# An eight-batch attention and expert tower on one core: queries and keys projected three heads ahead instead of two, in the third and fourth unit of a head

## What is computed

```python
q  = concat(qn, rope(qr))            # per head 32 + 64, from the latent cq
k1 = concat(kn, rope(kr))            # causal branch, kr shared by the heads
ks = rope_part(sel @ Wsel_k)         # 128 selected tokens
kw = rope_part(x @ Wwin_k)           # window of 128 tokens
o  = g0 * attn(q, k1, causal) + g1 * attn(q, ks) + g2 * attn(q, kw, causal & window)
out = o.reshape(B, T, NH * VD) @ Wproj
```

## Time and profile before

| | us |
|---|---|
| median of three runs (1845.43 to 1846.01) | 1845.62 |
| the profiled execution, its own time | 1848.94 |
| its span | 1847.0 |
| PE busy in the span | 1430.7 (77%) |
| DVE busy | 1437.1 (78%) |
| ACT busy | 1222.9 (66%) |
| POOL busy | 1434.9 (78%) |
| POOL's share of the chain that ended last | 58% |
| from one batch's transfer of latents to the next's, six times (191.02 to 191.58) | 191.2 |

### The profile page before, as it was taken

How to read it: one execution, slowest core, us unless ns; L and a number is a source line. 1 busy time by engine, 2 the same in 40 slices (tenths; PEclk the granted TensorE clock), 3 DMA queues, 4 the chain that set the end, 5 groups by cost and what they waited for, 6 DMA issues and landing times.

```text
span 1847.0 us, 64237 instructions
## 1 busy us (share of the span) xinstructions
PE 1430.7 (77%) x19368; PEld 1152.9 (62%) x19368; DVE 1437.1 (78%) x4982; ACT 1222.9 (66%) x3280; POOL 1434.9 (78%) x2126
## 2 busy tenths in 40 slices
PE   1041488888888888888888888888888888888778
PEld 0021377767776777777777767677767776766643
DVE  5737588877888788878887888788878887878845
ACT  0041378767777777768776777687768776767634
POOL 6775489877887798779887998698868887889710
PEclk9985699999999999999999999999999999999989
DMA  5110232313222322222222222222222221333200
GB/s 92 22 26 2 47 63 51 58 38 65 54 54 41 65 53 51 44 61 52 58 50 55 53 55 51 54 51 55 55 50 55 51 57 38 55 64 68 53 4 21
DMA packets 327554, 92.04 MB, mean 50 GB/s; under 512 B 321104, under 2 KB 323024, under 8 KB 327520
## 3 DMA queue, kind: packets, MB, share of 16 engines
q1 hardware_dynamic: 324448, 88.48, 24.3%
q0 software_dynamic: 3072, 3.15, 1.0%
HBM read 6.51 MB, written 1.05 MB: 4 GB/s over the span
## 4 chain that ended last, share of the span: by engine, by line
POOL 58%; issue 20%; DVE 8%; PE 7%; POOLq 3%; DMA 2%; ACT 1%; DVEq 0%; ACTq 0%; SPq 0%
POOL big L425 10%; POOL big L424 8%; POOL kparts L460 6%; POOL big L394 5%; POOL vh L480 4%; POOL kparts L457 4%; POOL qparts L446 4%; POOL kk L428 3%; POOL kk L429 3%; POOL qs L428 3%; POOL qs L429 3%; POOL osum L473 2%; DVE S L1008 2%; DMA qh<-qparts 1%; DVE big L1018 1%
## 5 line engine op out<-in xcount | busy, mean ns | idle before, releaser
L635 ACT ACTIVATE big<-S,negm 128x128 f32<-128x128 f32 (+3 forms) x1536 | 575.9, 448 | 209.3 <-DVE negm L1008 208.9
L647 ACT ACTIVATE big<-PT 128x384 f16<-128x384 f32 (+3 forms) x1024 | 426.7, 454 | 133.0 <-PE PT L1373 98.4
L1018 DVE SCALAR_TENSOR_TENSOR big<-PT,big 128x384 f16<-128x384 f32 (+3 forms) x1024 | 472.1, 500 | 32.5 <-ACT big L647 18.7
L1008 DVE CUSTOM_DVE_ANT_0 S<-S,mask_c,unscale 128x128 f32<-128x128 f32 (+3 forms) x512 | 285.0, 557 | 179.4 <-PE S L1348 167.5
L1348 PE MATMUL S<-k1T,qh 128*128 128x128 f16 (+3 forms) x1536 | 298.6, 304 | 117.2 <-DMA qh<-qparts 107.9
L1348 PE MATMUL S<-kh,qh 128*128 128x128 f16 (+1 forms) x3072 | 324.5, 243 | 0.0
L1395 PEld LDWEIGHTS O<-vh,big 128*128 128x128 f16 x8064 | 274.0, 96 | 46.0 <-DVE big L1030 28.5
L1395 PE MATMUL O<-vh,big 128*128 128x33 f16 x8064 | 283.7, 178 | 19.6 <-DVE big L1030 16.3
L1348 PEld LDWEIGHTS S<-kh,qh 128*128 128x128 f16 x3072 | 231.2, 100 | 56.9 <-issue 1.4
L1380 PE MATMUL PT<-cst,big 128*128 128x128 f32 x1408 | 249.3, 282 | 18.8 <-DVE big L1018 16.1
L1373 PE MATMUL PT<-cst,big 128*128 128x128 f32 x1280 | 233.6, 282 | 18.6 <-DVE big L1018 18.2
(11 more groups left out here) (295 smaller groups left out, 2395.5 us busy)
## 6 DMA issues: line engine op xcount, KB each, us to landing
lat_b<-lat_all SPq DMA_DIRECT2D x8, 448.0 KB, 3.1
qh<-qparts SPq DMA_TRANSPOSE x128, 3.0
kh<-kparts SPq DMA_TRANSPOSE x128, 3.3
xnT_all<-xnT_b SPq DMA_DIRECT2D x14, 128.0 KB, 2.5
xn_b<-xn_all SPq DMA_DIRECT2D x8, 128.0 KB, 2.8
xnT_b<-xnT_all SPq DMA_DIRECT2D x8, 128.0 KB, 2.3
out_dram<-h_all SPq DMA_DIRECT2D x8, 128.0 KB, 2.0
xn_all<-xn_b SPq DMA_DIRECT2D x7, 128.0 KB, 2.0
```

The lines of the kernel that those rows point to most:

```text
L635: last = nc.scalar.activation(pr[par][:, lo:lo + n], S[par][:, lo:lo + n], ACT.Exp, bias=negm[par][:, k:k + 1], scale=-1.0)
L647: last = nc.scalar.activation(pT[par][:, 0, lo:lo + n], PT[:, lo:lo + n], ACT.Copy, scale=PSCALE)
L1008: last = v.tensor_tensor_reduce(out=z, in0=z, in1=m, scale=unscale[:] if k == 0 else kfix[:], scalar=3.0e38, op0=ALU.add, op1=ALU.min, acc ...
L1018: v.scalar_tensor_tensor(pT[par][:, 1, lo:lo + n], PT[:, lo:lo + n], PSCALE, pT[par][:, 0, lo:lo + n], ALU.mult, ALU.subtract).then_inc(s[ ...
```

## The change

`LEAD` gets two more entries, the queries and keys of head 2 (`qp2`, `kp2`). They are projected at the end of the batch before: the queries in unit 3 of its last turn, the keys in `behind` between the scores of the first block and the transposes of the attention's output. In the first batch both stand in `behind`. Inside a batch, turn h now projects head h + 3: its keys in unit 2, its queries in unit 3, and ACT copies them out first in those units; `high_values` moves from unit 2 to unit 1. The loops of PE and ACT take one pair of turns less, and turns 12 and 13 are written out behind them; turn 13 projects nothing. GpSimd does its work in the same order as before, only grouped otherwise in its loop, except that `normalise` in the last batch now stands behind `low_values` and `branch_sum`. DVE and SP are unchanged.

```diff
-        LEAD = ["cq", "qp0", "sel", "k1", "kp0", "qp1", "kp1"]
-        NX = (NH - 2) * 2 + len(LEAD)
+        LEAD = ["cq", "qp0", "sel", "k1", "kp0", "qp1", "kp1", "qp2", "kp2"]
+        NX = (NH - 3) * 2 + len(LEAD)
...
+            def cycle(b, h, par, rows=None, add=True):
                 x = xbase(b) + h * 2
+                low_values(par, b, h + 1)
+                if add:
+                    branch_sum(par, b, h - 1)
                 if rows is not None:
                     normalise(rows, xn_b[:])
-                low_values(1 - par, b, hh - 1)
+                prepare(par, b, h + 3, x + x_index(0, "kp"), x + x_index(0, "qp"))
...
             def heads(b, rows=False):
+                prepare(0, b, 2, xbase(b) + x_lead("kp2"), xbase(b) + x_lead("qp2"))
+                cycle(b, 0, 1, 0 if rows else None, add=False)
                 with g.Fori(0, NH // 2 - 2) as hp:
+                    cycle(b, hp * 2 + 1, 0)
+                    cycle(b, hp * 2 + 2, 1, hp + 1 if rows else None)
+                low_values(0, b, NH - 2)
...
# ACT, turn
-                    if t == 0 and last < 1:
-                        evac_k(p, xb + x_index(0, "kp"), H + 1)
-                    if t == 1 and last < 1:
-                        evac_q(p, xb + x_index(0, "qp"), H + 1)
-                    if t == 2 and last < 2:
+                    if t == 1 and last < 2:
                         high_values(1 - p, b, h + 1)
+                    if t == 2 and xb is not None:
+                        evac_k(1 - p, xb + x_index(0, "kp"), H + 2)
+                    if t == 3 and xb is not None:
+                        evac_q(1 - p, xb + x_index(0, "qp"), H + 2)
...
# PE, turn
-                    if last < 1 and t == 0:
-                        k_proj(h + 2, xb + x_index(0, "kp"))
-                    if last < 1 and t == 1:
-                        q_proj(h + 2, xb + x_index(0, "qp"))
+                    if xb is not None and t == 2:
+                        k_proj(h + 3, xb + x_index(0, "kp"))
+                    if xb is not None and t == 3:
+                        q_proj(h + 3, xb + x_index(0, "qp"))
...
# PE, behind
                 scores(0, 0, 0, H * NT)
+                if first:
+                    lead("qp2", b, nxt)
+                lead("kp2", b, nxt)
```

More of the change, by code:

```diff
@@ L523, in weight_parts, with prepare @@
                 last.then_inc(s["comb_ready"], 1)
-            def prepare(b, h, hh, par, rows=None):
+            def prepare(par, b, hh, xk, xq):
+                key(par, b, hh, xk)
+                query(par, b, hh, xq)
+            def cycle(b, h, par, rows=None, add=True):
                 x = xbase(b) + h * 2
-                key(par, b, hh, x + x_index(0, "kp"))
-                query(par, b, hh, x + x_index(0, "qp"))
+                low_values(par, b, h + 1)
+                if add:
+                    branch_sum(par, b, h - 1)
                 if rows is not None:
                     normalise(rows, xn_b[:])
-                low_values(1 - par, b, hh - 1)
+                prepare(par, b, h + 3, x + x_index(0, "kp"), x + x_index(0, "qp"))
             def heads(b, rows=False):
-                prepare(b, 0, 2, 0, 0 if rows else None)
+                prepare(0, b, 2, xbase(b) + x_lead("kp2"), xbase(b) + x_lead("qp2"))
+                cycle(b, 0, 1, 0 if rows else None, add=False)
                 with g.Fori(0, NH // 2 - 2) as hp:
[L537 to L541, removed]
+                    cycle(b, hp * 2 + 1, 0)
+                    cycle(b, hp * 2 + 2, 1, hp + 1 if rows else None)
+                low_values(0, b, NH - 2)
                 branch_sum(0, b, NH - 4)
@@ L706, in lead @@
                 elif kind[:2] == "qp":
-                    evac_q(int(kind[2]), x, H)
+                    evac_q(int(kind[2]) % 2, x, H if kind != "qp2" else H + 1)
                 elif kind[:2] == "kp":
-                    evac_k(int(kind[2]), x, H)
+                    evac_k(int(kind[2]) % 2, x, H if kind != "kp2" else H + 1)
             def behind(b, nxt, U, first):
@@ L724, in behind @@
                 probs(0, 0, b, U)
+                if first:
+                    lead(LEAD.index("qp2"), nxt, b * NH)
+                lead(LEAD.index("kp2"), nxt, b * NH)
                 if not first:
@@ L729, in behind @@
                 probs(2, 2, b, U + 2)
-            for i in range(len(LEAD)):
+            for i in range(LEAD.index("qp2")):
                 lead(i, 0)
@@ L737, in heads @@
             def heads(b, rows=False):
-                with act.Fori(0, NH // 2 - 1) as hp:
+                with act.Fori(0, NH // 2 - 2) as hp:
                     for p in range(2):
                         turn(b, hp * 2 + p, xbase(b) + hp * 4 + p * 2, p, 0, rows=hp if rows and p == 1 else None)
+                turn(b, NH - 4, xbase(b) + (NH - 4) * 2, 0, 0)
+                turn(b, NH - 3, None, 1, 0, rows=NH // 2 - 2 if rows else None)
             def last_heads(b, nxt):
@@ L1492, in heads @@
             def heads(b, rows=False):
-                with pe.Fori(0, NH // 2 - 1) as hp:
+                with pe.Fori(0, NH // 2 - 2) as hp:
                     for p in range(2):
@@ L1496, in heads @@
                              rows=hp if rows and p == 1 else None)
+                turn(NH - 4, b * NH + NH - 4, xbase(b) + (NH - 4) * 2, 0, 0)
+                turn(NH - 3, b * NH + NH - 3, None, 1, 0, rows=NH // 2 - 2 if rows else None)
             def hidden(b, chunks=(0, 1, 2, 3), between=None):
@@ L1517, in _ @@
             last.then_inc(s["rank_psum"], 1)
-            for kind in LEAD[2:]:
+            for kind in LEAD[2:LEAD.index("qp2")]:
                 lead(kind, 0, 0)
```

## The result

The changed kernel takes 1905.39 us (median of four runs, 1903.54 to 1946.84) against 1845.53: slower, with a ratio of 1.0321 and a 95% interval of 1.0303 to 1.0339. The sign that was forecast and its mechanism, the queries on the chain, are there; the size is not: 59.9 us instead of 26, and the range ended at 1898.

The account below looks back on a forecast made before the run. GpSimd was taken to bound the kernel mid-batch, with the PE, ACT and DVE chain bounding it afterwards. Heads +19, last batch -3 and clock +10 gave +26 on 1848.9, so 1875, or 1872 against the median; range 1838 to 1898.

Parts of the forecast that it names:

- the queries on the chain: Unit 3 on PE: twelve matmuls between `values` and `scores` lengthen the chain through PE, ACT and DVE by 0.74 us.
- What bounds the kernel: Mid-batch, GpSimd sets the pace, busy 9.87 of 10.97 us a head; PE's 107.9 us wait for queries is its lateness.
- The head: One head inside a batch: 10.53 + 0.74 - 0.10 = 11.17 us, longer than GpSimd's 10.97.
- the base of 10.53: Mean length in us of two second-batch heads that GpSimd did not hold, taken as what PE, ACT and DVE need.
- Keys in unit 2: Key projection on PE ahead of unit 2's scores: hidden while `take_hi` holds DVE; taken as 0, bounds 0 and 0.50 us.
- The clock: Ten lower-clock stretches in heads of the first seven batches, 1.9 us each, no longer hidden by GpSimd: 10 us, bounds 0 and 19.
- every second head: Rival: PE's waits in units 0 and 1 make the clock fall in 45 heads, 86 us, 1948 us; chance 0.05.
- Between batches: `kp2` and `qp2` around the end of a batch: hidden by PE's later wait for GpSimd's sums; 0, at most 5.8 us.
- The last batch: GpSimd, which also normalises, stays the limit there; its one wait of 2.89 us can go: taken as -2.9.
- The sum: Whole kernel: 19 - 3 + 10 = +26 us on the profiled 1848.9, giving 1875, or 1872 against the median.
- GpSimd stays the limit: Rival: queries in unit 3 are hidden, heads stay 10.97, GpSimd's waits at batch starts go: -32, 1814 us; chance 0.15.
- The balance rival: Half the queries' time is hidden, a head takes about 10.98 us: 1844 us; below 11.0 the change gains; chance 0.10.

Follow-up runs that it names:

- units01_rolled: Changed kernel with keys projected in unit 0, queries in unit 1, values' copy in unit 2, and turns 12 and 13 back in the loops: 1823.3 us.
- queries1_rolled: Changed kernel with queries back in unit 1, values' copy in unit 3, keys left in unit 2, turns 12 and 13 back in the loops: 1837.6 us.
- queries_later: Changed kernel with turns 12 and 13 back in the loops, unit 3's queries behind its scores and transposes, their copy behind `take_hi`: 1810.7 us.
- later_long: Changed kernel with only unit 3's queries and their copy one step later; turns 12 and 13 stay written out: 1880.2 us.
- units01: Changed kernel with keys projected in unit 0, queries in unit 1, values' copy in unit 2; turns 12 and 13 stay written out: 1891.7 us.

## Why the prediction was wrong in size

**What bounds the kernel**: right. PE's wait for the queries was GpSimd's lateness; it went, and the time went elsewhere.

**The head**: the mechanism was right, and its term nearly so. 11.17 was forecast; heads without a fall take 11.03 in the changed kernel, 11.05 in the one with added work. The queries on the chain cost 0.68 a head (11.05 against 10.37, the mean of the first nine heads in units01_rolled) where 0.64 was put; the base of 10.53, from two heads of the second batch, was 0.16 too long. Since GpSimd held a head at 10.97 before, 0.06 to 0.08 of the 0.68 reaches the time of a head. Keys in unit 2, put at 0, cost at most 0.18 (2.4 in thirteen heads, in queries1_rolled) and nothing that queries_later shows. Wide `maxima` 11.1 to 11.4 apart were to be seen; they are 10.83 and 11.23 apart in turn.

**The clock**: mis-sized. "Ten such stretches", 10 us in all, took the count of the trace before. The count is what changed: 28 instead of 11 in the heads. The 1.9 us put for one was too much: one costs 1.38 us in the pair shown above; against the kernel with the added work they cost 4.1 us a batch, some 25 in six batches. The prediction had the mechanism among its rivals (every second head, 1948 us, chance 0.05) and should have put a lower rate of it into the forecast: the waits that the moved projections leave in units 0 and 1 were named there. The Trainium skill ("TensorE: Matmul & The Clock Gate", "A second HAM failure mode: psum-queue depth-cycling") tells of a kernel in which short idle times between groups of matmuls come often enough to make the clock go up and down; the trace agrees, with waits of 0.85 and 0.66 us ahead of the fall shown.

**Between batches**: this is the step that failed outright. "0, at most 5.8" was worked out for `kp2` and `qp2`, and for those it holds: 24.2 with them and the short program, 24.7 before. That the change writes two turns out stands in the description of the change, and no term was put for it. It costs 25 us over the ways in the changed kernel, of which 21 show against the kernel before, and 33 in all where nothing else is changed. The Trainium skill ("Runtime: NRT & Kernel Launch", "Instruction fetch mechanics") says that a branch taken to a place that is not among the instructions kept makes the engine fetch them, in blocks of 16 KiB, before it goes on; the runs agree, with 79 or 80 packets of 16.3 KB on average (1.29 MB / 79) and idle times of 4.67 and 5.42 us. A loop of 634 matmuls stays, one of 918 is loaded again; where between them the limit lies, no run here shows.

**The last batch**: -2.9 forecast, -0.4 measured. The wait of 2.89 is gone there, but GpSimd's normalising now stands behind other work, and PE waits 17.2 us for its rows where it waited 11.4; the clock also falls four times in the heads of this batch instead of once. What each of the two takes back was not parted.

**The sum**: of the 53.1 us up to the last wide `maxima`, the chain makes some 10 (34.4 in the heads less 25), the falls some 25, the ways between batches 21; the start, the first and the last batch together take 2.3 off. The forecast had 19, 10 and 0 for the three. With the program short again the chain and its falls alone still make the kernel slower (1894.4), so the direction was no luck; more than four fifths of the loss came from the two terms that were put too low.

**The rivals**: "GpSimd stays the limit", 1814 us, came out in its number as soon as the queries left the chain and the program was short again: 1810.7. Its mechanism came out in part. In the batch from 975.16 GpSimd waits 1.2 us for copies of keys, where it waited 8.0 in the kernel before, and PE waits for the transposed queries again (37.2 us in all, 31 times); but a head, which was to stay at 10.97, takes 10.6 on average. So that -32 was forecast and -35 measured is in part luck. The changed kernel loses this gain to the queries' place, to the lower clock that this place brings, and to the written-out turns. The balance rival put its point at a head of 11.0. By the length of a head at full clock the changed kernel lies on that point (11.03), and is decided by what the rival left out. The Trainium skill's rule of the most-contended engine ("Perfetto Trace Analysis", "Identifying the Most-Contended Engine"), which the prediction names with the first rival, picks GpSimd within a head (9.87 of 10.97 us busy) and so the right wait to remove; it doesn't tell what the removal may cost elsewhere.

What stays open: which waits of PE bring a fall and which don't (queries_later keeps a wait of 0.70 in unit 1 and has two); what of the 84 us comes from the projection on PE and what from its copy on ACT, which moved together; and why later_long and units01 take 133 us behind the last wide `maxima`.

## What to carry to other kernels

Before a step is moved on an engine, find the result there that others wait for, and put the step behind it: twelve matmuls ahead of the scores or behind them, with their copy, make 84 us here. When a change writes turns of a loop out, read the instruction queue's line on the page and count the loop's instructions: the price here was paid at every return to the loop's start, as idle time of that engine. And a wait of PE can cost more than its length: 0.85 and 0.66 us stand ahead of a fall that costs 1.38, so count the falls that a change may bring, not those that are there.

## What the runs showed of the hardware

TensorE loads instructions again at every return to the start of a loop that is too long for it: 64 packets more over six returns, 1.04 MB, and 4.67 and 5.42 us of idle time at the two that are shown, with a stretch at 0.50 from the idle time on. Work added to TensorE makes the kernel faster where it fills waits: 1894.4 to 1856.5 us for twenty-two matmuls more in a head. And the lower clock can last: 102.75 us at 0.50 while PE is busy for 101.11 of them; what holds it there is open.
